# Order of a few ACT instructions in the first gate unit, and of SP's transfers around the LoRA-B rows, in a two-layer fp32 kernel

## The reference, cut to what matters

```
y  = mixture-of-experts 1x1 conv of x (weights from cond), + bias      # layer 0, y bias
x1 = x + y @ kernel + bias + LoRA(y)        # LoRA: rank 32, own A and B for each of 8 groups, and a shared A and B
c  = grouped conv (9 taps) of x1 + cond term + bias                     # layer 1
h  = silu(c @ w12a.T + b12a) * (c @ w12b.T + b12b)
out = x1 + h @ w3.T + b3
```

## Time and profile before

| | |
|---|---|
| median of 3 runs | 801.6 us (801.58 to 801.7) |
| profiled execution, its own time | 800.24 us |
| its span in the trace | 798.4 us |
| PE busy | 777.2 us (97%) |
| DVE busy | 526.6 us (66%) |
| ACT busy | 207.0 us (26%) |
| POOL busy | 84.6 us (11%) |

### The profile page before, as it was taken

How to read it: one execution, slowest core, us unless ns; L and a number is a source line. 1 busy time by engine, 2 the same in 40 slices (tenths; PEclk the granted TensorE clock), 3 DMA queues, 4 the chain that set the end, 5 groups by cost and what they waited for, 6 DMA issues and landing times.

```text
span 798.4 us, 10404 instructions
## 1 busy us (share of the span) xinstructions
PE 777.2 (97%) x3889; PEld 655.3 (82%) x3889; DVE 526.6 (66%) x636; ACT 207.0 (26%) x251; POOL 84.6 (11%) x57
## 2 busy tenths in 40 slices
PE   5998899999999999989999999999999999999998
PEld 4877788888888899968888888888888888888886
DVE  4767676355363469987777759877755896555552
ACT  2531011001000032233333337333333731111110
POOL 4150462422313000000000000000000000000000
PEclk9999899999999999999999999999999999999999
DMA  8967665455484899244445133278862754444441
GB/s 225 286 177 228 170 170 130 127 116 150 111 172 120 182 270 239 81 131 132 131 138 161 43 126 138 80 227 235 240 246 79 261 213 158 160 175 165 158 172 64
DMA packets 88380, 131.47 MB, mean 165 GB/s; under 512 B 11208, under 2 KB 66936, under 8 KB 85656
## 3 DMA queue, kind: packets, MB, share of 16 engines
q1 hardware_dynamic: 85136, 129.90, 55.7%
q10 hardware_dynamic: 3064, 0.90, 0.6%
q0 software_dynamic: 144, 0.21, 0.1%
HBM read 78.20 MB, written 51.72 MB: 163 GB/s over the span
## 4 chain that ended last, share of the span: by engine, by line
PE 85%; SPq 6%; DVE 5%; DMA 4%; issue 1%; ACT 0%; DVEq 0%
PE ps L1836 37%; PE ps L1595 30%; PE ps L1896 18%; SPq L400 2%; DVE cr L1299 1%; DMA raw<-in_L_ffn_kernel 1%; DMA lora_b_scratch<-lb_c_lo 1%; SPq L439 1%; DMA h_f<-h_scratch 1%; SPq L356 1%; DMA lb<-lora_b_scratch 1%; SPq L366 1%; DVE lb_c_lo L1159 1%; DVE w_a_f L1249 1%; DVE wk_lo L1070 0%
## 5 line engine op out<-in xcount | busy, mean ns | idle before, releaser
L1836 PE MATMUL ps<-cr,w_s_hi 128*128 128x512 f32 x512 | 159.0, 392 | 3.4 <-ACT s L921 3.4
L1836 PE MATMUL ps<-cr,w_a_hi 128*128 128x512 f32 x384 | 118.3, 389 | 0.0
L1836 PEld LDWEIGHTS ps<-cr,w_s_hi 128*128 128x128 f32 x512 | 96.6, 189 | 24.5 <-issue 4.5
L1836 PE MATMUL ps<-cr,w_s_lo 128*128 128x512 f32 x256 | 100.1, 391 | 0.0
L1836 PEld LDWEIGHTS ps<-cr,w_a_hi 128*128 128x128 f32 x384 | 71.9, 188 | 14.9 <-issue 0.2
L1595 PE MATMUL ps<-wk_hi,y_hi 128*128 128x512 f32 x256 | 80.5, 395 | 0.0
L1595 PE MATMUL ps<-wk_lo,y_hi 128*128 128x512 f32 x256 | 79.1, 390 | 0.0
L1595 PE MATMUL ps<-wk_hi,y_lo 128*128 128x512 f32 x256 | 78.9, 389 | 0.0
L745 POOL TENSOR_TENSOR x_t<-x_in,f_bias 128x1024 f32<-128x1024 f32 x16 | 63.6, 3981 | 136.9 <-DMA x_scratch<-x_t 136.9
L1147 DVE TENSOR_TENSOR x_t<-ps,x_t 128x1024 f32<-128x1024 f32 x16 | 19.5, 1223 | 88.3 <-PE ps L1595 88.3
L1836 PE MATMUL ps<-cr,w_a_lo 128*128 128x512 f32 x192 | 74.7, 389 | 0.0
(11 more groups left out here) (177 smaller groups left out, 1242.0 us busy)
## 6 DMA issues: line engine op xcount, KB each, us to landing
x_scratch<-x_t SPq DMA_DIRECT2D x128, 64.5 KB, 2.1
x<-x_scratch SPq DMA_DIRECT2D x32, 258.0 KB, 6.9
x_in<-in_x SPq DMA_DIRECT2D x16, 512.0 KB, 6.5
r_scratch<-r_t SPq DMA_DIRECT2D x16, 512.0 KB, 3.2
h_scratch<-s SPq DMA_DIRECT2D x32, 256.0 KB, 2.4
h_f<-h_scratch SPq DMA_DIRECT2D x8, 1024.0 KB, 5.9
res<-r_scratch SPq DMA_DIRECT2D x16, 512.0 KB, 5.1
raw<-in_L_ffn_w SPq DMA_DIRECT2D x56, 128.0 KB, 4.4
```

What stands on the lines that cost most here:

```text
L1836: last = pe.matmul(o, l, r, start=first and q == 0 and n == 0, stop=q == 3 and n == 2, skip_group_check=True)
```

## The change

In the first gate unit, ACT's list begins with the copies of partial sums 0 and 1, and copy 2 stands between the two roundings `a_hi` of the next unit's weights; the rest of the unit keeps its order. The other units are as they were. On SP, x tile 2 is loaded first (without the wait for the seventh `wk_lo`), then the y bias, and then tile 3; the stores of the B rows to `lora_b_scratch` are halved: SP issues the four of the first rank half ahead of b3, ACT those of the second half right behind its own `first_group_lb`. x tile 5 is loaded behind the rows of group 1.

```
+        def store_lb(eng, pair):
+            eng.wait_ge(lora_taken, N_LORA)
+            for hl in range(2):
+                for odd in range(2):
+                    eng.dma_start(lb_w[hl, odd, pair], lb_c[hl][pair][64 * odd:64 * odd + 64, :]).then_inc(lb_stored[pair], 16)
...
-            wait_slot(sp, raw_of(KT - 2))
-            load_x(3, 3)
             sp.wait_ge(taps_mm, 1)
             load_x(2, 2)
             sp.wait_ge(yb_stored, 16)
             sp.wait_ge(lbs_stored, 32)
             sp.wait_ge(lb_shared, 64)
             sp.dma_start(y_bias[:, QUART:], ...).then_inc(bias_rest_loaded, 16)
+            wait_slot(sp, raw_of(KT - 2))
+            load_x(3, 3)
             first_group_lb(sp, 0)
+            store_lb(sp, 0)
             wait_slot(sp, raw_of(7))
             sp.dma_start(b3_s[:, :], b3.partition_broadcast(P)).then_inc(b3_in, 16)
-            sp.wait_ge(lora_taken, N_LORA)
-            for pair in range(2):
-                for hl in range(2):
-                    for odd in range(2):
-                        sp.dma_start(lb_w[hl, odd, pair], lb_c[hl][pair][64 * odd:64 * odd + 64, :]).then_inc(lb_stored[pair], 16)
...
             sp.wait_ge(xb_made, 2)
-            for t in (4, 5):
-                load_x(t, t - 4)
+            load_x(4, 0)
             for pair in range(2):
                 sp.wait_ge(lb_stored[pair], 64)
             sp.wait_ge(lb_loaded[0], LB_FIRST[0])
             load_lb(1, group_lb(NG), 2 * RANK)
             load_lb(1, group_lb(1), 0)
+            load_x(5, 1)
...
             first_group_lb(act, 1)
+            store_lb(act, 1)
             split_y(2, 1, 0)
...
             act.wait_ge(c_taken, 8 + NB)
-            for u in range(HALF_UNITS - 1):
+            part_copy(0, 0)
+            part_copy(0, 1)
+            a_hi(1, 0)
+            part_copy(0, 2)
+            a_hi(1, 1)
+            silu(0, 0)
+            s_hi(1, 0)
+            s_hi(1, 1)
+            silu(0, 1)
+            for u in range(1, HALF_UNITS - 1):
                 gate_unit(u)
```

## The result

| | before | changed |
|---|---|---|
| median of 6 runs each, same chip | 801.75 us (801.58 to 802.28) | 806.43 us (805.05 to 807.29) |
| ratio | | 1.0061, 95% interval 1.0051 to 1.0072 |
| span of the profiled execution | 798.4 us | 804.6 us |

What follows compares the result with a forecast made beforehand. PE was taken as the bound, with three waits of 8.2 us together. First phase 0.9 + 2.9 + 2.8 = 6.6 gained, gate unit 1.2 lost: -5.4 us, median 801.6 to 796.2, range 794.3 to 799.2.

Steps and rivals of the forecast that it cites:

- y bias, 0.9 gained: First phase: y bias lands before DVE needs it, so y_f of tile 2 starts without its 0.88 us idle; 0.9 gained.
- Stores, landing 69.3, bounds 67.0 to 72.6: First phase: stores of B rows land at 69.3, not 75.6, so PE's wait for group 1 goes; 2.9 us gained.
- the second bound: First phase: if ACT's half of the stores is worth nothing, SP's start 3.0 us earlier and land at 72.6.
- the 2.9 for the wait: First phase: PE's wait for the LoRA B rows of group 1 disappears, 2.9 us gained.
- the 2.8 for the clock: First phase: without the long wait PE stays at full clock from restart to u_tile(3), 4.5 us not 7.26; 2.8 gained.
- What is late next: First phase, z_group(2): y_lo of tile 5 ready at 95.6, PE there at 96.1; slack 0.5 us, nothing counted.
- Gate unit, 1.2 lost: Gate unit 0: wait of 3.4 before t3 becomes 4.8 before t4, half clock there costs 1.6; 1.2 us lost.
- Sum: Whole kernel: first phase -6.6, gate unit +1.2, together -5.4 us, 0.7%; median from 801.6 to 796.2.
- The third: Stores land at 70 to 73 and z_group(2) or group 1 loads wait, 798.1; or gate clock costs 2.8, 797.4; chance 0.20.
- The slower one: First phase: stores overtake SP's group 0 copies, u_lora(0) waits, PE pays 2.8 for the clock; 804.6 us; chance 0.04.
- the prediction's own signs of being wrong: Stores landing after 72, a wait for y_lo or z at z_group(2), a wait of u_lora(0), or t4 starting near 348.

Runs made afterwards that it cites:

- the hold: One added wait: POOL's addition of tile 4 waits for y_lo of tile 5; changed kernel with it 801.70 and 801.11 us, kernel before with only it 800.98.
- the last batch: Runs on one chip: kernel before 801.42 us, changed kernel again 805.04, changed kernel with the hold 801.11, kernel before with only the hold 800.98.
- the y-bias kernel: Kernel before with only SP's loads reordered to x tile 2, y bias, x tile 3, all stores still on SP: 799.42 us, ratio 0.9975.

## Why the prediction was wrong, by its own steps

- **y bias, 0.9 gained: right.** The bias was issued at 42.97, earlier than the 47.5 worked out, and y_f of tile 2 started at 61.05, not 61.91. PE was at its wait for group 1 at 79.77; 79.7 was worked out.
- **Stores, landing 69.3, bounds 67.0 to 72.6: mis-sized, and outside the bounds.** They landed at 73.7. The estimate counted bytes at 0.147 MB per us from 47.5 on, whoever issues and whatever the shape. But x tile 3 was issued only at 49.95, and the stretch from 54 to 58, with the 8-row copies first in both queues, moved 73 GB/s at a share of 0.52, where 58 to 66, with the stores, had 163 GB/s at 0.48. The shares fit the half of the engines that was assumed; the rate within it did not hold. That the shape sets this rate is argued, not tested. The issuing was mis-sized too: SP's four stores were out at 65.8 and ACT's at 61.7, not at 61.3 and 59.4. And ACT's half was worth nothing that can be told: with all stores on SP and the bias early they landed at 73.8 and by 74.2 (the kernels with y bias), and in the eight executions with ACT's half at 73.0 to 76.0, where the second bound said 72.6. The rule that the prediction cited from the Trainium skill (DMA: Bandwidth & Descriptors, "Issuing engines are not separate DMA queues") agrees with this. So the 2.9 for the wait did not come (3.2 is left), nor most of the 2.8 for the clock: from the restart to u_tile(3) it took 5.9, where 7.3 was before and 4.5 was counted. At u_tile(3) 1.9 was gained and not 6.6.
- **What is late next: this step failed, and it turned the sign.** It took POOL's start plus 14.7 as the time of y_lo of tile 5, and "DVE gets its y_lo of tile 4 in before POOL starts" as the point where the loss ends. The 14.7 was read from an execution with POOL first; it became 16.9 (87.14 to 104.01). POOL's own start was late too, 13.4 behind the stores' landing, where 11.6 was counted. With DVE first the additions land elsewhere: the first pair is short, and the next addition comes 3.5 earlier, onto the y_lo that sets `z_group(2)`. The meeting cost a wait of 3.15 and 2.7 of half clock behind it (16 products in 3.55 and not 1.91, `y_tile(6)` 2.75 and not 1.71). Forcing that order without the change gave 806.31; the hold took 5.7 from that kernel and 3.9 from the changed one.
- **Gate unit, 1.2 lost: right in mechanism, mis-sized.** t4 began 10.4 after t1's end (10.3 worked out) behind a wait of 4.93 (4.8). The clock cost 2.5 in t4 and not 1.6, inside its bound of 2.8: 2.2 lost in the traces, 1.8 by the runs. The 1.6 came from t3 before, whose wait was shorter (3.4).
- **Sum.** -1.9 at u_tile(3), +6.0 at `z_group(2)`, +2.2 in the gate unit: +6.3, where the spans differ by 6.2. By the runs of the last batch: +3.9 for the meeting, -0.3 for all the rest, together 3.6, what that batch shows between the two kernels. The six runs of the result showed 4.7.
- **Rivals.** The third named the place (`z_group(2)`) and nearly the landing (70 to 73), but priced the loss at 1.9 and kept it faster. The slower one had another mechanism, `u_lora(0)` waiting, which did not come. None had POOL's addition of tile 4 on the y_lo of tile 5. Two of the prediction's own signs of being wrong did come: a landing after 72, and a wait for y_lo at `z_group(2)`.

**Open:** what decides the order by some tenths. Against the kernel before, y_lo of tile 4 came 0.9 earlier and POOL's start 0.5 later, though its stores were issued 1.07 earlier (77.92, not 78.99). Nor is it known what makes these stores slow to land: x tile 5, now ahead of them, would be a cause, but with it back in its old place POOL still began 9.4 behind their first issue (9.2 in the changed kernel, 7.7 in the kernel before). That is one execution, so it is not ruled out.

## What to carry to other kernels

When a change moves work by tenths of a microsecond, look at every pair of engines that start within about a microsecond of each other and slow each other: which comes first there is part of the schedule, and a slack read from one execution holds for that order only. Fix such an order with a wait on the engine that has time to spare; here one wait on POOL was worth 3.9 us to the changed kernel and nothing that can be told to the kernel before. Price a wait on the bounding engine with its half-clocked work behind it, and by the longest such stretch that the trace has.

## What the runs showed of the hardware that was not expected

- **DVE and POOL hold each other off for whole instructions, and the first to start decides.** In all 16 profiled executions in which nothing forced the order, DVE's pair of y_lo of tile 4 took 6.8 to 8.5 us when POOL's first addition had begun first (nine executions), and 1.47 to 4.98 when y_lo had begun first (seven; 1.47 where its lead was 0.79 or more, so that both were through); a lead of 0.03 to 0.06 us was enough (85.56 against 85.59, 87.08 against 87.14). The Trainium skill (SBUF — State Buffer, section "Who interferes with whom") says that a DVE instruction with two SBUF inputs contends with a GpSimd instruction that reads SBUF, and that who issues first keeps the other out until it is done. The traces agree: y_lo (two SBUF inputs) is held off, `take_x1`, which reads one input from PSUM, takes 1.21 to 1.23 beside POOL, and `residual`, which reads two from SBUF, takes 4.55 beside POOL and 2.18 without. The prediction did not use this rule.
- **The clock.** It fell to 0.50 behind waits of 2.9 to 4.9 us, behind one of 2.19 (0.50 from 84.0 to 85.5 in the changed kernel with the hold), and once behind 1.91 (1.00 at first, then 0.50 from 84 to 86 in the y-bias kernel), where 1.90 had cost nothing before. Behind 4.93 it stayed for 5.25 us. Matmuls into an unused bank kept it at 1.00 (4.69 us of them in the gate unit).
- **8-row copies.** At about half of the transfers' share, 73 GB/s were moved while they stood first in the queues, and 163 with the 64-row stores behind them; the two were not measured apart.
